# Query and key parts of a gated attention unit: one product with three copies each and five row moves, in place of two products with six copies

## The reference

```python
q, k, v = elu(conv1d_valid(x, W) + b)            # kernel width 3, so 748 tokens; 8 heads of 16
h = softmax(q @ k.T / 4) @ v                     # token attention
nx = layer_norm(layer_norm(h))                   # the gated unit normalises again
q, k, linear, pre_gelu = split(nx @ expand)      # widths 16, 16, 256, 256
gated = linear * gelu(pre_gelu)
local, v = gated[:, :128], gated[:, 128:]
mask = where(causal, sigmoid(rel + position_bias_mult), -inf)
attn = softmax(q @ k.T / 4 + mask) @ v
h = h + layer_norm(h) + concat(local, attn) @ project
h = h + moe(layer_norm(h))                       # router of 64 experts, top 2, capacity 128; one shared FFN of 512
```

## Time and profile before

| | |
|---|---|
| median of three runs | 804.38 us |
| profiled execution, its own time | 804.39 us |
| profiled execution, span | 802.7 us |
| mean granted TensorE clock | 0.994 |
| PE busy | 778.9 us, 97% of the span |
| DVE busy | 674.7 us, 84% |
| ACT busy | 504.3 us, 63% |
| POOL busy | 288.6 us, 36% |
| second block | 528.2 us to the end, rounds of some 33 us |

### The profile page before, as it was taken

How to read it: one execution, slowest core, us unless ns; L and a number is a source line. 1 busy time by engine, 2 the same in 40 slices (tenths; PEclk the granted TensorE clock), 3 DMA queues, 4 the chain that set the end, 5 groups by cost and what they waited for, 6 DMA issues and landing times. The chain is left out here.

```text
span 802.7 us, 15609 instructions
## 1 busy us (share of the span) xinstructions
PE 778.9 (97%) x5555; PEld 475.5 (59%) x5555; DVE 674.7 (84%) x1608; ACT 504.3 (63%) x1100; POOL 288.6 (36%) x291
## 2 busy tenths in 40 slices
PE   9899999999999999999999999999999999999997
PEld 5354564564564564564563343367878788787785
DVE  3797998999899899899899889648788887787956
ACT  3275776776777677677677677655554636546333
POOL 4355241241342342342644245312436342333222
PEclk9799999999999999999999999999999999999999
DMA  4509143143143145135125300010000000000001
GB/s 112 78 18 122 11 61 85 15 62 84 15 63 83 15 57 88 15 53 92 16 44 81 67 7 5 9 14 8 2 21 1 20 20 2 21 1 20 20 2 38
DMA packets 85676, 31.08 MB, mean 39 GB/s; under 512 B 58496, under 2 KB 84320, under 8 KB 85600
## 3 DMA queue, kind: packets, MB, share of 16 engines
q1 hardware_dynamic: 85024, 29.61, 22.4%
q10 hardware_dynamic: 576, 0.49, 0.4%
HBM read 4.76 MB, written 3.06 MB: 10 GB/s over the span
## 5 line engine op out<-in xcount | busy, mean ns | idle before, releaser
L464 ACT ACTIVATE probs<-ps_a 128x384 f32<-128x384 f32 (+1 forms) x732 | 301.0, 480 | 129.1 <-PE ps_a L668 126.7
L552 DVE TENSOR_REDUCE neg_max<-ps_a 128x1 f32<-128x512 f32 (+1 forms) x384 | 247.9, 677 | 39.6 <-PE ps_a L684 36.1
L668 PE MATMUL ps_a<-q_rep,k_rep 98*128 98x384 bf16 (+3 forms) x768 | 231.8, 324 | 1.7 <-DMA q_rep<-max_T 1.0
L684 PE MATMUL ps_a<-k_rep,q_rep 96*128 96x512 bf16 (+3 forms) x768 | 218.3, 327 | 8.0 <-DVE neg_max L552 4.9
L699 PE MATMUL ps_pv<-probs,v_hat 128*32 128x364 f32 (+3 forms) x1536 | 135.6, 482 | 1.2 <-DVE out_r L531 0.6
L668 PEld LDWEIGHTS ps_a<-q_rep,k_rep 98*128 98x128 bf16 (+1 forms) x768 | 77.3, 102 | 94.9 <-issue 37.7
L684 PEld LDWEIGHTS ps_a<-k_rep,q_rep 96*128 96x128 bf16 (+1 forms) x768 | 75.1, 103 | 86.9 <-DVE neg_max L552 27.0
L554 DVE TENSOR_REDUCE neg_max<-ps_a 128x2 f32<-128x472 f32 x192 | 122.7, 639 | 0.0
L699 PEld LDWEIGHTS ps_pv<-probs,v_hat 128*32 128x32 f32 (+1 forms) x1536 | 42.7, 109 | 60.9 <-issue 40.5
L2009 POOL TENSOR_TENSOR out_n<-out_r,inv_sum 128x192 f32<-128x192 f32 x32 | 16.3, 511 | 157.4 <-DVE inv_sum L533 149.2
L279 POOL TENSOR_SCALAR qk_e<-qk_e 128x748 f32<-128x748 f32 x14 | 38.0, 2714 | 25.7 <-ACT qk_e L370 25.7
(11 more groups left out here) (239 smaller groups left out, 1182.3 us busy)
## 6 DMA issues: line engine op xcount, KB each, us to landing
k_rep<-parts_k SPq DMA_DIRECT2D x96, 96.0 KB, 3.8
q_rep<-parts_q SPq DMA_DIRECT2D x93, 96.0 KB, 4.0
hall<-out_n SPq DMA_DIRECT2D x256, 12.0 KB, 1.8
xT<-in_x SPq DMA_DIRECT2D x8, 375.0 KB, 3.7
out_h<-y_out SPq DMA_DIRECT2D x7, 320.0 KB
q_rep<-max_T SPq DMA_DIRECT2D x32, 6.0 KB
w_sb<-in_w_T SPq DMA_DIRECT2D x2, 256.0 KB, 3.5
out_h<-y_out SPq DMA_DIRECT2D x8, 54.0 KB
```

The source lines that it names most:

```text
L464: act.activation(probs[0:rows(kt), n % RING, 0:w], ps_a[0:rows(kt), 3 + n % 3, 0:w], ACT.Exp, scale=DH ** -0.5).then_inc(p_ready, 1)
L552: dve.tensor_reduce(neg_max[0:rows(t), 0, col:col + 1], ps_a[0:rows(t), c, :], AX.X, ALU.max, negate=True).then_inc(sc_max, 1)
L668: pe.matmul(out[0:rows(kt), 0:QW[qh]], k_rep[0:KM, cb % 2, h, kt * P:kt * P + rows(kt)], q_rep[0:KM, cb % 2, qh, h, 0:QW[qh]], start=True, ...
L684: last = pe.matmul(out, q_rep[0:KS, it % 2, t // QT, h, t % QT * P:t % QT * P + rows(t)], k_rep[0:KS, it % 2, h, 512:L] if c == 2 else k_r ...
```

## The change

For the sequences 1 to 7 one product now gives queries and keys. Its stationary operand `qk_w3` holds three copies of the query columns and three of the key columns, again 96 rows. The parts are made once on these 96 rows (rows 0 to 47 queries, high, middle, low; rows 48 to 95 keys), by one `high`, one `left`, one `middle` and one `rest`, with factors `take_3`. Five transfers in SP's queue then copy groups of 16 to 48 rows to their places in `qk_rep`, which has two buffers for alternate sequences. In the order, `qk` moves ahead of `scores_T` 0; `high` stands behind `exponential` 0 and `middle` behind `exponential` 3; `left` stands behind `weigh` 0 and `rest` behind `weigh` 4. In round 0 `qk` stands between the third and the fourth row tile of `attend`, and `left` and `rest` ahead of `attended`. `order_of` follows, so the banks of nearly all products change. Also, DVE's last turn of the token attention's outputs moves behind the meeting of the blocks, POOL makes eight more small constants in the first block, and DVE two more small copies. The diff, cut (sequence 0 keeps its old way; `take_3` is made by a memset and six `affine_select`):

```diff
-    qk_rep = sb("qk_rep", [KM, 2, LP], BF16)
+    qk_rep = sb("qk_rep", [KM, 2, 2, LP], BF16)
+    qk_w3 = sb("qk_w3", [P, 2, 3, QK], F32)
+    take_3 = sb("take_3", [KS, 2], F32)
-    N_MADE = 24
+    N_MADE = 32
...
     def scores(pe, o, n, t):
-        if t == 0:
-            pe.wait_ge(S["x_rep"], n * 2 + 2)
+        if t == 0 and n == 0:
+            pe.wait_ge(S["x_rep"], 2)
+        elif t == 0:
+            pe.wait_ge(S["x_spread"], 80 * n)
...
         add(y, it, ("attend", 0, 2))
-        add(x, it + 1, ("qk", 0, 2), ("qk", 1, 2))
+        add(x, it + 1, ("qk", 0, 2))
...
     add(z, it - 1, ("ffn1", 2, 2), ("ffn1", 3, 2))
+    add(x, it + 1, ("qk", 0, 2))
     add(y, it, scores_T[0])
     add(z, it - 1, ("ranks", 0, 1))
     add(y, it, *scores_T[1:3])
     add(z, it - 1, ("ffn2", 0, 1))
     add(y, it, *scores_T[3:5])
-    add(x, it + 1, ("qk", 0, 2))
     add(y, it, scores_T[5])
-    add(x, it + 1, ("qk", 1, 2))
     add(y, it, ("attend", 0, 2))
...
+        def spread_qk(n):
+            def move(j, at, src):
+                sp.dma_start(qk_rep[at:at + src.shape[0], n % 2, j, 0:L], src).then_inc(S["x_spread"], 16)
+
+            if n > 1:
+                sp.wait_ge(S["y_st"], (n - 1) * NT)
+            sp.wait_ge(S["x_part_a"], n)
+            move(0, 0, part_a[0:3 * QK, 0, :])
+            move(1, 5 * QK, part_a[5 * QK:6 * QK, 0, :])
+            sp.wait_ge(S["x_last"], n)
+            move(0, 3 * QK, part_a[0:3 * QK, 1, :])
+            move(1, 0, part_a[3 * QK:6 * QK, 1, :])
+            move(1, 3 * QK, part_a[3 * QK:5 * QK, 1, :])
+
         for it in range(B + 1):
             if it >= 2:
                 store(it - 2)
+            if 0 < it < B:
+                G["rows_of_max"](sp, it)
             if it == 0:
                 spread(sp, B - 1, 0)
+            if it + 1 < B:
+                spread_qk(it + 1)
+            if it == 0:
                 spread(sp, B - 1, 1)
-            elif it < B:
-                G["rows_of_max"](sp, it)
...
+        def high(n):
+            act.wait_ge(S["x_qk"], n)
+            if n > 1:
+                act.wait_ge(S["x_spread"], 80 * (n - 1))
+            act.copy(in_two(part_a[:, 0, :]), halves("qk", n)[0:KS]).then_inc(S["x_part_a"], 1)
+
+        def middle(n):
+            act.wait_ge(S["x_left"], n)
+            act.copy(part_b[:, 0, :], left_a[:, 0, :]).then_inc(S["x_part_b"], 1)
...
                 for k in range(NT):
                     exponential(it, k)
-            if x:
-                high(it + 1, 0)
-                high(it + 1, 1)
+                    if x and k == 0:
+                        high(it + 1)
+                    if x and k == 3:
+                        middle(it + 1)
...
     def _(dve):
+        turn_outputs(dve, ps_pv, B - 1, 3)
         dve.memset(table[:, :], 0.0).then_inc(setup, 1)
...
+        def left(n):
+            dve.wait_ge(S["x_part_a"], n)
+            dve.scalar_tensor_tensor(in_two(left_a[:, 0, :]), in_two(part_a[:, 0, :]), take_3[:, 0:1], halves("qk", n)[0:KS],
                                      ALU.mult, ALU.add).then_inc(S["x_left"], 1)
...
+        def rest(n):
+            dve.wait_ge(S["x_part_b"], n)
+            dve.scalar_tensor_tensor(part_a[:, 1, :], part_b[:, 0, :], take_3[:, 1:2], left_a[:, 0, :],
+                                     ALU.mult, ALU.add).then_inc(S["x_last"], 1)
...
                 for k in range(NT):
                     weigh(it, k)
+                    if x and k == 0:
+                        left(it + 1)
+                    if x and k == 4:
+                        rest(it + 1)
...
-            if x:
-                left(it + 1, 0)
-                left(it + 1, 1)
             if y:
                 attended(it)
             if z and it < B:
                 transform(it - 1, 1)
-            if x:
-                rest(it + 1, 0)
-                rest(it + 1, 1)
...
+        def qk(n):
+            o = take("qk", n, 0, "x_left", n)
+            pe.wait_ge(S["x_nx2T"], n + 1)
             for h in range(2):
-                last = pe.matmul(o[0:KS, 512 * h:512 * h + HALF], qk_w[:, j, :, :].rearrange("p a c -> p (a c)"),
+                last = pe.matmul(o[0:KS, 512 * h:512 * h + HALF], qk_w3[:, :, :, :].rearrange("p j a c -> p (j a c)"),
                                  nx2T[:, h * HALF:(h + 1) * HALF], start=True, stop=True)
             last.then_inc(S["x_qk"], 1)
...
                 ffn1(it - 1, 3)
+            if x:
+                qk(it + 1)
             if y:
                 scores_T(it, 0)
```

More of the change, by code:

```diff
@@ L860, in _ @@
             last_step(s, probs_step(B, s))
+    return ps_pv
 QK = 16
@@ L1124, in scores @@
             diag = b == w
-            last = pe.matmul(o[0:rows(t), a:b], qk_rep[0:KS, 0, t * P:t * P + rows(t)], qk_rep[0:KS, 1, a:b],
+            last = pe.matmul(o[0:rows(t), a:b], qk_rep[0:KS, n % 2, 0, t * P:t * P + rows(t)], qk_rep[0:KS, n % 2, 1, a:b],
                              start=True, stop=not diag)
@@ L1251, in gated_units @@
     nx2T, part_a, left_a, part_b, qk_rep = (G[n] for n in "nx2T part_a left_a part_b qk_rep".split())
+    qk_w3, take_3 = (G[n] for n in "qk_w3 take_3".split())
     gel = sb("gel", [P, NT, P], F32)
@@ L1481, in _ @@
         turned_2(1)
-        for j in range(2):
-            high(1, j)
+        high(1)
+        middle(1)
         turned_att(0)
-        for j in range(2):
-            middle(1, j)
         for it in range(1, B + 1):
@@ L1703, in _ @@
                     local(it, j)
+                left(it + 1)
+                rest(it + 1)
+                attended(it)
                 G["normalise"](dve, it + 2)
-                attended(it)
-                for j in range(2):
-                    left(it + 1, j)
-                for j in range(2):
-                    rest(it + 1, j)
                 sum_2(it)
@@ L1834, in scores_T @@
                 diag = a == 0
-                last = pe.matmul(o[0:rows(k), a:b], qk_rep[0:KM, 1, k * P:k * P + rows(k)], qk_rep[0:KM, 0, k * P + a:k * P + b],
+                last = pe.matmul(o[0:rows(k), a:b], qk_rep[0:KM, n % 2, 1, k * P:k * P + rows(k)], qk_rep[0:KM, n % 2, 0, k * P + a:k * P + b],
                                  start=True, stop=not diag)
@@ L1840, in scores_T, with attend @@
             last.then_inc(S["y_st"], 1)
-        def attend(n):
+        def attend(n, between=None):
             o = take("attend", n, 0, "y_norm", n + 1)
@@ L1845, in attend @@
             for t in range(NT):
+                if between and t == 3:
+                    between()
                 pe.wait_ge(S["y_p"], n * NT + t + 1)
@@ L1924, in _ @@
         turn_2(1)
-        attend(0)
-        for j in range(2):
-            qk(1, j)
+        attend(0, lambda: qk(1))
         turn_att(0)
```

85 lines of the change are left out of this document (33 added, 52 removed).

## The result

The changed kernel takes 818.4 us (median of four runs: 817.5, 819.3, 812.3, 819.2); the kernel before took 804.3 beside it. The ratio is 1.016, 95% interval 1.011 to 1.021: slower, as forecast, 3.9 us above the 814.5 of the prediction and inside its range. The four runs lie 7 us apart, where those of the kernel before lie within 2; the one of 812.3 had a mean granted clock of 0.995, the others 0.984. The profiled run is one of the longer ones: 817.53 us, its span 815.8.

The account below looks back on a forecast made before the run. PE, busy 97%, was taken as the bound, with the hidden 3, table load, Exp, `weigh` path almost level late in a round. Rounds +11.1, turn of the blocks -0.9, round 0 -0.1: +10.1 on 804.4 gives 814.5 us, range 806 to 825.

Parts of the forecast that it names:

- The new wait: PE ahead of `ffn2` 0: idle 2.35 us for `left`, last reader of the reused `qk` bank, in rounds 1 to 6.
- A plain round: Rounds without POOL's delay: each loses 1.0 us; rounds 4 and 5 together +2.0, round 6, without `normalise`, +0.84.
- POOL's chain: Rounds 1 and 2: reciprocal 4.14 us later delays POOL's statistics and the next `turn_3`; +3.5 and +4.1 us.
- Round 3: +0.7 us: `ranks` waited for `chosen` there before, 0.3 of it now filled by `qk`.
- The turn of the blocks: Between the blocks: DVE's transpose and reciprocal, moved behind the meeting, leave the path; -0.9 us.
- Round 0: PE saves 1.28 us, but `sum_2` and its normalisation set the round's end; -0.1 us, bounds -1.3 to +0.7.
- Transfers at nothing: SP's five transfers behind the parts: 0, as they land before `scores` needs them; without that cover 4 us per round.
- POOL's constants: First block: eight constants, some 2.7 us, beside PE's work; with DVE's copies costed 0, at worst +0.7 us.
- DVE's two copies: First block: two small copies beside PE's work; with POOL's constants costed 0, at worst +0.7 us.
- rival 1: Clock falls in the new gaps: four falls of 2 to 4.5 us, 822 to 832, say 826 us; chance 0.14.
- Rival 2: POOL and DVE catch up, so rounds 1 and 2 lose as plain ones: +5.7 - 1.0, 809 us; chance 0.14.
- Rival 3: At `ffn2` 0 `left` is not waited for; six rounds win 1.28 us plus old wait: 795.7 us; chance 0.08.

Follow-up runs that it names:

- a_warm: Changed kernel with two float32 products, results unread, filling PE's idle time ahead of `ffn2` 0 in rounds 1 to 6; 813.38 us, ratio 1.0118.
- before_again: The kernel before, unchanged, run and profiled once more; 804.17 us, ratio 1.0000.
- b_turn: The kernel before with only the last turn of the token attention's outputs moved into the second block; 803.20 us, ratio 0.9986.
- b_const: The kernel before with only POOL's eight more constants in the first block, results not used; 802.07 us, ratio 0.9977.
- old_places: a_banks with late constants, `high`, `middle`, `left`, `rest` back near their old places, two bank entries different; 802.06 us, ratio 0.9965.
- a_banks: Changed kernel with only eight bank entries of rounds 1 to 6 handed out anew, `ffn2` 0 taking the bank of `ranks`; 801.35 us, ratio 0.9959.
- the second median of 814.3: The changed kernel, unchanged, in a second set of four executions; median 814.3 us, ratio 1.0114.
- a_hole: a_banks with `normalise` behind the attended values (798.02 us), plus a wait for `left` ahead of `ffn2` 0, no bank behind it; 813.47 us.

## Why the prediction was right, and where it was not

**The new wait: right.** 2.35 us forecast, 2.16 measured, in six rounds, put down to `left` through the bank. `attend` 4.96 became 4.91 and no longer waits. From the first product behind `ffn1` 3 to the reciprocal it is 687.05 - 672.54 = 14.51 us after, and was 672.74 - 663.89 = 8.85; less the 1.6 that `ffn2` 0 lost at the lower clock, the reciprocal stands 4.1 us later, against 4.14 forecast. A plain round, +1.0 forecast: +1.01 in round 5, +0.96 in round 6 (34.04 against 33.08; forecast 0.84), +1.18 in round 4 with the hole filled.

**POOL's chain: near for round 2, too high for round 1.** Round 2: +3.7 for 4.1. Round 1: +2.0 without the fall, for 3.5. The idle time ahead of the two `turn_3` behind these rounds was to be 2.4 us; it is 0.92 and 1.80, and 1.80 and 1.79 in a_warm. The step that failed is that POOL's chain keeps its length. From `prob` to the end of `rs_zr` it took 584.99 - 571.17 = 13.8 us before and 588.17 - 575.94 = 12.2 after; in round 2 12.9 and 12.2. Two of the statistics steps were long before, beside DVE's `rest`, and 0.20 us each after, when `rest` stood elsewhere. POOL and DVE in the kernel before:

```profile
576.12 0.98 POOL L1051 TENSOR_TENSOR rs_all<-rs_v,rs_all 128x6 f32<-128x6 f32 x1
577.17 0.83 POOL L1053 TENSOR_TENSOR rs_v<-rs_all 128x6 f32<-128x6 f32 x1
```
```profile
576.05 1.89 DVE L1671 SCALAR_TENSOR_TENSOR qk_rep<-part_b,take_out,left_a 96x748 bf16<-96x748 bf16 x2
```

The first of the two in the changed kernel:

```profile
581.03 0.20 POOL L1050 TENSOR_TENSOR rs_all<-rs_v,rs_all 128x6 f32<-128x6 f32 x1
```

The Trainium skill ("GPSIMD Engine Reference", section "1. Specifications") says that GpSimd shares its way into SBUF with VectorE and contends with VectorE instructions that read two inputs from SBUF. `rest` is such an instruction, and the rows agree. No run was made for this, but the traces tell: in all four profiles of kernels with the old pairs (before, before_again, b_turn, b_const) the two steps stand beside `rest` and take 0.98 or 0.99 us and 0.82 or 0.83 us; beside DVE's `h`, which reads one of its inputs from PSUM, they take 0.20. In old_places, where `rest` is back behind the attended values, it meets an earlier step of POOL, and both are longer, 1.60 for 0.99 and 1.57 for 1.00:

```profile
571.07 1.60 DVE L1726 SCALAR_TENSOR_TENSOR part_a<-part_b,take,left_a 96x748 bf16<-96x748 bf16 x1
```
```profile
571.96 1.57 POOL L1428 TENSOR_TENSOR is<-is 128x384 f32<-128x384 f32 x1
```

**Round 3: right** (0.7, measured 0.72 with the hole filled). The six rounds together: 11.1 forecast, 1.98 + 3.71 + 0.72 + 1.18 + 1.01 + 0.96 = 9.6 measured.

**The turn of the blocks: right.** -0.9 forecast; the marks go from +0.82 at the last transpose that both have in the first block to -0.06 at the first `scores_T` after, 0.9 less, and b_turn gives -1.05. Round 0: -0.1 forecast, -0.1 measured (the first `turn_3` at 553.02, from 553.18, less the 0.06 that the first `scores_T` has already). **Transfers at nothing: right**; the time per plain round in a_banks is PE's.

**Costed at nothing, wrong:** POOL's constants. "0, at worst +0.7" was 1.1 for them (0.57 of it one hole in PE at 406 us). The cover that I named, PE's work beside them, does not hide it: PE waits there for DVE's `neg_max`, an instruction of its own loop. For DVE's two copies no cost is shown. The marks slip by 0.6 us between 450 and 464 us in the profile after, where the copies stand, but by 0.4 in before_again, which has no copies, and by nothing in a_warm, which has them. A fall of the clock at 428 us added 1.4 in the profiled execution. All this did not show in the total, as its first 80 us were 2.4 us shorter than in the profile that I took for the sum.

**The clock: mis-sized.** This is the term of the sum that was put at nothing and was not. I gave it to rival 1, with a chance of 0.14, since the clock had held at 1.5 us of idle at the turn of the blocks. That was one execution: before_again has the same 1.50 us there and a clock of 0.61 behind it. It falls in three or four of six rounds, as the rival said, but costs 1.4 to 1.6 us (rounds 3 and 4: 35.54 and 35.80 against 34.13 and 34.26), and 0.8 in round 1 of the first profile, where PE waits for POOL's chain anyway. The rival's 2 to 4.5 us was too dear, and its 826 never appeared. Forecast and rival were the same mechanism with and without an addition. The eight executions fall into three groups, by their mean clock: 812.0 and 812.3 (0.995), 814.1 and 814.6 (0.991), and 817.5 to 819.7 (0.984). The falls in the rounds are 3.8 and 6.1 us in the two that were profiled, both of the third group; in the others they were not seen.

The Trainium skill ("TensorE: Matmul & The Clock Gate", section "Why this matters for your kernels") warns against idle gaps between bursts of matmuls that are longer than these holes. By that rule the holes of 2.16 us would be harmless. Here 11 of the 18 in three profiles were not, and the measurement decides.

**Luck in the total.** For the profiled execution the account is 9.6 us for the rounds, 3.8 for the falls in them, -1.0 for the turn and round 0, and +0.8 for the first block (-2.4, +1.1, +1.4 and +0.6): 13.2, and the spans differ by 13.1. The forecast had 10.1. That the first block comes to +0.8 is chance, and that 814.5 is so near to the second median of 814.3 is chance too: its rounds were 1.5 us too dear, and it had neither the falls nor the constants.

**Rival 2** (POOL and DVE catch up, 809): 1.5 of the 2.5 us between rival and forecast in round 1, 0.4 of the 3.1 in round 2. **Rival 3** (no wait for `left`, 795.7) is what a_banks builds: 801.35. Its plain rounds did win, but 0.74 to 0.90 each, not 1.28: `ffn2` 0 waits 0.34 for the rank sums, `attend` takes 0.24 more to the next product's start, and in round 4 `logits` begin 0.13 later. Round 1 won nothing, and round 2 lost 1.7 to POOL's chain.

## What to carry to other kernels

When work is moved ahead on the engine that bounds the kernel, look up which buffer each following instruction reuses and who read it last: here eight entries of a bank table decide between a loss of 1.1 to 1.6% and a gain of 0.4%, with every instruction the same. Price a new hole in TensorE's work by its length, and give it a second term for the clock behind it, with a spread, since that term comes and goes between executions. "Beside PE's work" is no cover if the engine in question feeds that work in the same loop; read its idle time there before writing 0.

## What was not expected of the hardware

- Of the twenty idle times of 2.16 us or more inside the rounds of four profiles (six each in the two profiles after and in a_hole, two in old_places), twelve had the granted clock fall to half behind them; of fifteen between 1.5 and 1.8 us in the two profiles after, a_banks and a_warm, none had. The 1.50 us at the turn of the blocks had it once in two profiles of one program. So had a shorter one: an idle time of 1.13 us at 427 us stands in all thirteen profiles, and the clock fell behind it in two, after and a_banks (0.57 and 0.60 from 428 to 432 us). The length of the idle time alone does not tell, therefore, whether the clock falls.
- The same program's profile can lose or win 1.5 us in its first 60 us: in before_again the early half clock began and ended some 2 us earlier than in before (0.74 from 24 to 28 us and 0.98 from 36 to 40, against 0.98 and 0.74), and in b_const it lasted less long; no change in the second block should be read from a span without setting the marks of the first against each other.
- POOL's operations on 6 columns took 0.98 and 0.83 us beside a DVE operation with two inputs in SBUF, and 0.20 without it.
